# Where an attention group's output leaves PSUM in a round: one transformer layer on one Trainium2 core

## The reference

```
x = conv_general_dilated(inputs, conv_w, 'SAME') + conv_b       # 3 taps, 1024 -> 768
q, k, v = split(x, 3)                                            # blocks of 128 tokens
qh, kh, vh = (q @ wq + bq, k @ wk + bk, v @ wv + bv)             # 16 heads of 64
scores = qh * scale @ kh.T, causal inside the block
p = softmax(scores)
o = p @ vh ;  o = o @ wo + bo ;  x = x + (o @ proj_w + proj_b)
```

## Time and profile before

| | |
|---|---|
| Time, median of 3 runs (lowest to highest) | 978.25 us (975.35 to 980.58) |
| The profiled execution's own time | 976.29 us |
| Its span, first to last instruction | 974.5 us |
| Mean granted clock of TensorE | 0.986 of full speed |
| Busy share of the span: PE, PEld, DVE, POOL, ACT | 93%, 71%, 71%, 47%, 43% |

### The profile page before, as it was taken

How to read it: one execution, slowest core, us unless ns; L and a number is a source line. 1 busy time by engine, 2 the same in 40 slices (tenths; PEclk the granted TensorE clock), 3 DMA queues, 4 the chain that set the end, 5 groups by cost and what they waited for, 6 DMA issues and landing times.

```text
span 974.5 us, 15517 instructions
## 1 busy us (share of the span) xinstructions
PE 907.2 (93%) x4992; PEld 695.5 (71%) x4992; DVE 694.1 (71%) x1449; ACT 418.8 (43%) x1127; POOL 454.3 (47%) x587
## 2 busy tenths in 40 slices
PE   4799999998999999999989999999999798999997
PEld 3477777775444787887777787887777676877785
DVE  5788887688998888455683686288289786776651
ACT  3534443421234336234773565367256443333331
POOL 1267777787763330000255255247144543555565
PEclk9899999998999999999999999999999998999999
DMA  9433322433234431864012124023244652444333
GB/s 283 182 130 130 130 87 88 144 127 109 98 103 156 162 119 44 313 227 173 1 44 65 44 56 141 1 77 96 94 91 139 212 198 86 145 134 149 130 108 108
DMA packets 43013, 119.98 MB, mean 123 GB/s; under 512 B 7232, under 2 KB 16448, under 8 KB 41536
## 3 DMA queue, kind: packets, MB, share of 16 engines
q1 hardware_dynamic: 42944, 119.11, 37.1%
HBM read 87.64 MB, written 31.46 MB: 122 GB/s over the span
## 4 chain that ended last, share of the span: by engine, by line
PE 70%; DVE 16%; issue 5%; ACT 4%; POOL 4%; DMA 1%; DVEq 0%; POOLq 0%; ACTq 0%
PE a_p_g L1925 19%; PE a_p_g L681 12%; PE f_p_m L681 9%; PE a_p_s L1949 4%; PE c_p_m L1353 3%; PE c_p_m L1355 3%; PE c_p_m L1354 3%; PE c_p_m L1351 3%; PE a_p_o L1973 3%; PE a_p_t L1959 2%; PE f_p_t L622 2%; DVE a_oT_lo L1852 1%; PE a_p_s L622 1%; ACT f_xT L549 1%; ACT a_s L1727 1%
## 5 line engine op out<-in xcount | busy, mean ns | idle before, releaser
L1653 POOL TENSOR_TENSOR a_s<-a_s,a_sums 128x512 f32<-128x512 f32 x64 | 66.6, 1041 | 232.9 <-DVE a_sums L1832 232.9
L309 POOL TENSOR_TENSOR f_y<-f_y,f_res 128x256 f32<-128x256 f32 x128 | 96.9, 778 | 114.8 <-DVE f_y L536 114.0
L1727 ACT ACTIVATE a_s<-a_s,a_nmx 128x128 f32<-128x128 f32 x256 | 99.5, 391 | 48.6 <-DVE a_nmx L1828 48.5
L681 PE MATMUL f_p_m<-f_wsign,f_a_hi 128*128 128x512 f32 x256 | 105.8, 413 | 0.0
L681 PE MATMUL a_p_g<-f_wsign,f_a_hi 128*128 128x512 f32 x256 | 103.2, 403 | 0.0
L681 PE MATMUL f_p_m<-f_wsign,f_a_lo 128*128 128x512 f32 x256 | 101.9, 398 | 0.0
L681 PE MATMUL a_p_g<-f_wsign,f_a_lo 128*128 128x512 f32 x256 | 101.1, 395 | 0.0
L299 POOL TENSOR_TENSOR f_res<-f_res,f_hbias 128x256 f32<-128x256 f32 x128 | 96.0, 771 | 0.0
L1925 PE MATMUL a_p_g<-c_xs_hi,x_room 128*128 128x512 f32 x256 | 94.7, 416 | 0.0
L1353 PE MATMUL c_p_m<-c_vh,c_ring 128*128 128x512 f32 x192 | 75.5, 393 | 5.3 <-issue 3.0
L1351 PE MATMUL c_p_m<-c_vf,c_ring_f 128*128 128x512 f32 (+1 forms) x192 | 73.8, 542 | 1.3 <-DVE c_ring_f L1019 1.1
(11 more groups left out here) (223 smaller groups left out, 2204.7 us busy)
## 6 DMA issues: line engine op xcount, KB each, us to landing
c_raw<-in_conv_w_dram SPq DMA_DIRECT2D x24, 768.0 KB, 4.3
f_w_raw<-in_w_t_dram SPq DMA_DIRECT2D x8, 1024.0 KB, 9.3
f_res<-in_x_dram SPq DMA_DIRECT2D x16, 512.0 KB, 3.9
x_after_ffn<-f_y SPq DMA_DIRECT2D x8, 1024.0 KB, 6.1
f_xin<-x_after_attention SPq DMA_DIRECT2D x8, 1024.0 KB, 5.0
f_res<-x_after_attention SPq DMA_DIRECT2D x16, 512.0 KB, 4.1
out_dram<-f_y SPq DMA_DIRECT2D x8, 1024.0 KB, 6.3
f_xin<-in_x_dram SPq DMA_DIRECT2D x7, 1024.0 KB, 5.2
```

What stands on the lines that cost most here:

```text
L309: last = pool.tensor_tensor(y[:, p, t, part], y[:, p, t, part], res[:, t, part], ALU.add)
L681: last = pe.matmul(p_m[:, q % 2, :], part[p][:, k, q // 2 * P:q // 2 * P + P], wsign[:, k, q % 2 * HALF:q % 2 * HALF + HALF], start=(k == ...
L1653: pool.tensor_tensor(s[:, r], s[:, r], sums[:, r].unsqueeze(2).broadcast_to([P, 4, P]), ALU.mult).then_inc(probs_ready, 1)
L1727: done = act.activation(s[:, r, h, :], s[:, r, h, :], ACT.Exp, bias=nmx[:, r, h:h + 1], scale=SCALE, accum_out=sums[:, r, h:h + 1])
```

## The change

Four edits, all in attention. (1) ACT takes the high part of a quad's output at the start of rounds 7, 11 and 15, ahead of that round's exponents (in round 15 behind the queries, which come first there); round 19 stays. (2) DVE takes the low part at the end of rounds 7, 11 and 15, that is ahead of the mask of rounds 8, 12 and 16, no longer at the end of 8, 12 and 16. (3) In round 16 DVE copies unit 13's probabilities ahead of unit 15's inverse instead of behind it and behind the round's keys. (4) In the last group POOL's bias of tile 3 moves from behind unit 12 to behind unit 10.

```diff
-LOW_ROUNDS = (8, 12, 16, 19)
+HIGH_ROUNDS = (7, 11, 15, 19)
+LOW_ROUNDS = (7, 11, 15, 19)
...
-                    if not first and u == (12 if last else 9):
+                    if not first and u == (10 if last else 9):
                         add_bias(g - 1, 3)
...
+            def attended(g, first, last, quad):
+                act.wait_ge(pv_done, UNITS * g + 4 * quad + 4)
+                if not first:
+                    act.wait_ge(gen_full, number(g, first, last, general(first, last)[0][0][0]))
+                for i in range(2):
+                    act.activation(oT[0][:, 2 * quad + i, :], p_o[:, i, :], ACT.Identity,
+                                   bias=bvs[:, 2 * quad + i:2 * quad + i + 1]).then_inc(o_hi, 1)
...
+                    if u < UNITS and u in HIGH_ROUNDS:
+                        attended(g, first, last, HIGH_ROUNDS.index(u))
                     if u < UNITS:
                         act.wait_ge(s_bias, UNITS * g + u + 1)
...
-                    if u >= V_LAG + 3 and (u - V_LAG - 3) % 4 == 0:
-                        quad = (u - V_LAG - 3) // 4
...
+                    if u >= UNITS and u in HIGH_ROUNDS:
+                        attended(g, first, last, HIGH_ROUNDS.index(u))
...
+            def copy_probs(g, w):
+                n = UNITS * g + w
+                dve.wait_ge(pt_full, n + 1)
+                wait(dve, pv_done, n - w % 2 - 2)
+                dve.tensor_copy(pt[:, w % SLOTS].rearrange("p h t -> p (h t)"), p_t[:, w % 2, :]).then_inc(pt_copied, 1)
...
+                    if u == UNITS:
+                        copy_probs(g, u - T_LAG)
                     if 1 <= u <= UNITS:
                         n, r = UNITS * g + u - 1, (u - 1) % SLOTS
                         dve.wait_ge(exp_done, n + 1)
...
-                    if T_LAG <= u < UNITS + T_LAG:
...
+                    if T_LAG <= u < UNITS + T_LAG and u != UNITS:
+                        copy_probs(g, u - T_LAG)
```

## The result

| kernel | median us | of runs | ratio to before, 95% |
|---|---|---|---|
| before | 977.53 | 4, 975.35 to 980.58 | |
| changed | 967.86 | 4, 964.98 to 970.69 | 0.9899 [0.9858, 0.9939] |
| changed, measured again | 970.32 | against 978.06 | 0.9909 [0.9893, 0.9925] |

The kernel is about 1% faster. The profiled execution took 968.3 us (span 966.5), 8.0 less than before's 976.3. The page shows how little of that is in the engines' shares: PE has the same work and loses some idle time. Span less busy time is 57.9 us, where it was 67.3. ACT's exponents wait 32.0 us; in the earlier trace rows they had waited 48.6.

A forecast was written before the change was run, and what follows sets the result against it. PE, busy 93%, bounds the kernel; its low-part waits total 11.5 us. Groups 0 to 3 gain 2.6 + 1.65 + 1.4 + 3.2 = 8.85, taking the profiled run from 976.3 to 967.5 and the median to 969.4, range 966 to 975.

The forecast's parts named there:

- group 0: Attention's first group: 1.15 from round 13, 0.67 from round 17 and 0.8 from the clock, 2.6 us in all.
- group 3: Last group, paced by DVE: 1.9 us earlier by round 15, 1.3 more from rounds 15 and 16, 3.2 in all.
- the clock's 0.8: Group 0 behind round 13's wait: the slow clock costs 1.58 us; with idle cut to about 2.0, half is won.
- Round 13 of groups 1 and 2: PE's 0.94 wait for the low part gives 0.5 us per group, 0.33 if all moves rigidly; the copy becomes last.
- a wait for the copy of 0.3 to 0.6: Sign of being right: PE shows this wait in round 13 of groups 1 and 2.
- DVE's stall of 0.43: Group 1, round 12: some 0.4 us in DVE's small instructions between mask and inverse, which may or may not recur.
- Round 17: Low part and copy come a microsecond early, so PE's waits go whole: 0.67, 1.26, 1.03 in groups 0 to 2.
- 0.1 for the values: End of groups 1 and 2: 0.1 us charged because next values need the low part fed by ACT's last cast.
- next group's values wait: Rival, chance 0.10: ACT's late last cast delays values ending groups 0 to 2, giving back 1.2 us each; 973.0.
- The copy takes over: Rival, chance 0.09: the copy becomes late everywhere; PE gains only DVE's filled idle, 3.6 us, nothing in round 17; 974.7.
- Slower: exponents late: Rival, chance 0.05: exponents' 1.24 delay reaches PE at all twelve moved places, costing 14.9 us; 6.0 slower, 984.3.
- slack of 0.8 to 1.2 in round 11 and 0.9 in round 15: Group 1: how much delay the exponents behind the high part can take, in us, before it reaches PE.

The follow-up runs named there:

- e2: Only unit 13's earlier copy and the earlier bias, on the kernel before; high and low part stay at their old places: ratio 1.0000 to before.
- e3: Only the high part moved ahead of the exponents, on the kernel before; low part, copy and bias as before: ratio 1.0072 to before.
- e1: Only high and low part moved, on the kernel before; copy and bias stay where they were: ratio 0.9951 to before.
- e8: Changed kernel, with the next group's first value product waiting for five of six input chunks, then for the sixth: ratio 0.9882 to before.
- a_again: The changed kernel itself, unaltered, measured and profiled a second time: 970.32 us against 978.06, ratio 0.9909 to before.
- e4: Changed kernel with POOL's bias of tile 3 put back behind unit 12 in the last group: ratio 0.9922 to before.
- e5: Changed kernel with a thrown-away query product in group 0's round 13, placed behind the wait for the copy: ratio 0.9904 to before.
- e7: Changed kernel with four small ACT copies (1.18 us) between high part and exponents in rounds 7, 11 and 15: 975.92 us, ratio 0.9977 to before.
- e11: Changed kernel with a thrown-away query product in group 0's round 13, placed ahead of the wait for the copy: ratio 0.9892 to before.
- e6: Changed kernel with group 0's first four products for the next group in rounds 13 to 16, not 14 to 17: ratio 0.9886 to before.
- e10: Changed kernel with both the values' wait in two steps and group 0's queries and keys a round earlier: ratio 0.9887 to before.

## Why the prediction was right, and where its terms were off

Forecast 969.4, range 966 to 975, measured 967.9. Forecast gain in the profiled execution 8.85, measured 8.0, of which 8.16 in attention and -0.16 outside it.

| | forecast | measured | again |
|---|---|---|---|
| group 0 | 2.6 | 1.67 | 3.09 |
| group 1 | 1.65 | 1.77 | 1.77 |
| group 2 | 1.4 | 1.51 | 1.50 |
| group 3 | 3.2 | 3.21 | 3.33 |

*Group 0.* The waits went as forecast: round 9's 0.4, and 2.75 became 1.86 where I had 2.0; round 17's 0.67 went, less 0.45 for the values. These give 1.5, against 1.15 + 0.67 = 1.8. The step that failed is the clock's 0.8, the half of 1.58. No profile shows a half: the rest, 1.67 and 3.09 less 1.5, is 0.2 in one and 1.6 in the other, nearly nothing and the whole. Over the study's profiles of group 0 the clock fell behind 2.75 in three of three (before, e2, e3), behind 1.86 in three of six (the changed kernel, e1, e8, not a_again, e4, e5), and not behind 2.17 (e7), 0.47 (e11) or 0.15 (e6, e10). What decides it at 1.86 stays open, and the length of the idle alone does not. That 0.8 lies near the mean of the two cases is luck; a reader should carry it as two cases. The Trainium skill, "TensorE: Matmul & The Clock Gate" ("HAM oscillation — how this bites in real kernels"), warns of oscillation where idles are long. Here shorter ones, 1.86 and 2.75, did it, the first in some executions of one kernel and not in others, and for this kernel the traces decide.

*Round 13 of groups 1 and 2.* I had 0.5, the copy taking the low part's place 0.33 in. The forecast sign, a wait for the copy of 0.3 to 0.6, did not come: 0.85 of the 0.94 went, and a wait of about 0.1 for the copy stays. The mask moved by the 0.98 that I had worked out (0.97 after taking the groups' offset of 0.40 off), but DVE's stall of 0.43 fell away. That was the term I had left to luck, and its cause is in the rows: the small instruction ended with POOL's in before. The same stall shows in group 3 of before and of e4 at 0.71. The Trainium skill, "SBUF — State Buffer" ("Who interferes with whom"), says that VectorE and GpSimd share one pair of ports as an exclusive lock; the traces agree for the negated maximum: 0.57 to 0.72 in the ten places of before where it starts beside POOL's work, and 0.17 in the other 54. DVE's inverse of the same size is not held up (0.16 to 0.18 everywhere, three times wholly within a POOL instruction). With that row read, the forecast would have been: the stall goes if POOL's low part ends first. As it was made, it was right in sign and the gain above 0.5 was luck.

*Round 17.* The copy at the inverse's place and the slack of the exponents held. I charged 0.1 for the values and 0.37 was due: exponents, inverse and POOL's product of round 15 are later, and POOL takes the last input low part only behind that product (598.38, its row above). ACT's cast is not to blame: it is through at 597.61, so 0.77 earlier. The rival "next group's values wait" named the right thing at a third of its price of 1.2, and by another way: POOL's own order, not ACT's cast. e8 shows that nothing else hangs on it: asked for in two steps, the wait gives 0.37 back. The two errors, +0.35 and -0.27, nearly cancel in each group, which is luck too.

*Group 3.* The sum was right, and so were its two stages: counted from the group's first scores, round 15's product comes 1.7 earlier where I had 1.9 (53.60 before, 51.87 now), and round 17's another 1.5 where I had 1.3 (59.02 and 55.82). What I put into the second stage was off. In e4, without the bias edit, the stages give 1.1 and 0.7 (52.49 and 57.18). The bias was priced at its wait of 0.69; it is worth 0.6 at round 15, and 0.7 more by round 17, because DVE's stall of 0.54 and POOL's late product go with it. High part, low part and copy together thus gave 0.7 in rounds 15 and 16, not 1.3. In round 17 PE still waits 1.20 for a copy; the 0.35 of round 19 stood there before, too. "The copy takes over" is thus true in group 3 and in round 13 of group 0, true by only 0.1 in round 13 of groups 1 and 2, and false in their round 17.

*Slower: exponents late.* The mechanism is real: e3 pays it where the low part is left behind (2.82 of wait at the inverse against 1.67, 0.7% slower), and e7 finds its edge between one and two high parts of delay. The forecast's slack of 0.8 to 1.2 in round 11 and 0.9 in round 15 was of the right size (0.76 and 0.74 measured); that the low part, moved too, delays the inverse by the same amount is what hides it.

## What to carry to other kernels

Where an in-order engine's work is late by order alone, move the whole chain: the high part alone cost 0.7%, high and low part together gained 0.5%, with copy and bias 1.0%. Read behind each removed wait what is due next on every queue that the product needs, here the copy and POOL's last low part. A wait for several inputs before an accumulation can be asked for piece by piece; it gave 0.37 us a group here in the trace, too little to be seen in the time.

## What the hardware showed

- At one place, behind the same idle of 1.86 us, in six profiles (the changed kernel twice, four variants with the same code up to there): TensorE's clock went to its lower level of 1.2 GHz in three and stayed at 2.4 GHz in three. Half speed cost 1.4 us where two profiles of one kernel can be compared. Behind a longer idle of 2.17 us at that place it stayed up in the one profile that has it, and behind 2.75 us it fell in three of three.
- In group 3 the clock fell behind several shorter waits in a row in three profiles (0.58, 0.75, 1.19 in e4; 0.55, 0.75, 1.30 in e1; 0.79, 0.75, 2.70 in e3), and in before, with 0.78, 0.75 and 1.93, it did not. Behind a single wait of 1.19 us that all thirteen traces have, it fell in two (e5, e7).
- VectorE's negated maximum (TENSOR_SCALAR, 128x4) takes 0.17 us, and 0.57 to 0.72 us where it starts while a GpSimd tensor operation runs; it then ends 0.02 to 0.03 us behind that operation. Where it starts behind GpSimd's end, it is free of that. RECIPROCAL of the same size takes 0.16 to 0.18 us either way.
